# Deformable attention and binary convolution on one core: another order of the first steps, thirteen product buffers, nine DMA sums and another order of projections

## What is computed

```python
# layer 1, deformable attention: 8 heads, 4 points, head size 8
q = x.reshape(B, C, Nq).transpose(0, 2, 1)
v = (q @ W_value + b_value).reshape(B, Nq, HEADS, d)
off = (q @ W_off + b_off).reshape(B, Nq, HEADS, LEVELS, POINTS, 2)
attn = softmax((q @ W_attn + b_attn).reshape(B, Nq, HEADS, POINTS), axis=-1)
loc = ref + off / norm                       # where each point samples v
sampled = bilinear sample of v at loc (0 outside the image)
out = (sampled.reshape(B, HEADS, d, Nq, POINTS) * aw).sum(-1)
x1 = (out @ W_out + b_out + q)               # back to (4, 64, 32, 32)
# layer 2, binary convolution
y = conv3x3(sign(x1 + move0_bias), mean(|w|) * sign(w), padding 1)
y = batchnorm(y) * gamma + beta              # mean and variance over the whole batch
y = prelu(y + x1 + move1_bias) + move2_bias
```

## Time and profile before

| | |
|---|---|
| median of three runs | 86.0 us (85.94 to 86.25) |
| the profiled execution | 85.9 us |
| its span, first to last instruction | 84.1 us |
| PE busy | 66.5 us, 79% |
| DVE busy | 58.7 us, 70% |
| POOL busy | 47.7 us, 57% |
| ACT busy | 46.2 us, 55% |
| mean granted clock of TensorE | 0.951 |

### The profile page before, as it was taken

The page is one execution under the profiler, slowest core; times in us unless marked ns, Lnnn a source line. Parts: engine busy times, 40 slices in busy tenths (PEclk is TensorE's granted clock), DMA queues, the critical chain, the costliest instruction groups (busy, mean ns, idle before and its releaser), DMA issues.

```text
span 84.1 us, 1712 instructions
## 1 busy us (share of the span) xinstructions
PE 66.5 (79%) x642; PEld 25.4 (30%) x642; DVE 58.7 (70%) x85; ACT 46.2 (55%) x92; POOL 47.7 (57%) x47
## 2 busy tenths in 40 slices
PE   5999997999799999999999959999799985200000
PEld 4766275223142322132323314222223542200000
DVE  2307978999989999596997889203970067689920
ACT  2401999995599999997000399900000397059500
POOL 7970000879999999999999999950000000009000
PEclk9999999999999999999999999999999999995555
DMA  0917865920599980091006638390000000000195
GB/s 9 295 42 253 250 232 123 224 74 0 97 207 213 213 146 1 0 216 37 0 8 134 119 53 134 64 189 4 0 0 0 8 0 0 0 4 0 24 281 194
DMA packets 3897, 8.09 MB, mean 96 GB/s; under 512 B 560, under 2 KB 1584, under 8 KB 3888
## 3 DMA queue, kind: packets, MB, share of 16 engines
q1 hardware_dynamic: 2320, 4.40, 19.1%
q0 software_dynamic: 1120, 2.88, 19.0%
q10 hardware_dynamic: 448, 0.69, 2.6%
HBM read 2.27 MB, written 1.05 MB: 39 GB/s over the span
## 4 chain that ended last, share of the span: by engine, by line
PE 50%; DVE 19%; POOL 10%; issue 8%; DMA 5%; ACT 2%; DVEq 1%; ACTq 0%; POOLq 0%
PE banks L530 21%; PE banks L513 12%; POOL ap L864 10%; DVE prod L970 6%; DMA win<-w_in_dram 5%; PE banks L562 4%; PE banks L476 3%; PE banks L508 3%; DVE prod L1104 3%; PE banks L459 2%; DVE prod L1115 2%; DVE bns L1075 2%; ACT sg L783 2%; DVE ays L941 1%; PE banks L466 1%
## 5 line engine op out<-in xcount | busy, mean ns | idle before, releaser
L864 POOL TENSOR_TENSOR ap<-ays,hat 128x512 f32<-128x512 f32 (+2 forms) x30 | 36.1, 1592 | 9.7 <-ACT hat L695 9.2
L970 DVE TENSOR_TENSOR prod<-banks,vpad 128x1024 f32<-128x1024 f32 (+2 forms) x20 | 22.1, 1114 | 8.2 <-PE banks L530 5.1
L530 PE MATMUL banks<-prod,wo 64*64 64x512 f32 (+2 forms) x208 | 23.1, 547 | 0.7 <-PE banks L530 0.5
L513 PE MATMUL banks<-ap,cst 32*64 32x512 f32 (+2 forms) x192 | 16.9, 567 | 1.5 <-POOL ap L864 1.0
L888 POOL TENSOR_SCALAR prod<-prod,prm,st 128x512 f32<-128x512 f32 x3 | 2.3, 763 | 19.8 <-ACT st L831 19.8
L970 DVE TENSOR_TENSOR prod<-banks,vswap 128x1024 f32<-128x1024 f32 (+3 forms) x13 | 12.6, 975 | 0.0
L530 PEld LDWEIGHTS banks<-prod,wo 64*64 64x64 f32 x208 | 6.9, 132 | 15.1 <-issue 11.1
L513 PEld LDWEIGHTS banks<-ap,cst 32*64 32x64 f32 x192 | 4.3, 130 | 13.7 <-POOL ap L864 8.1
L688 ACT ACTIVATE tab<-u,cst 128x512 f32<-128x512 f32 x12 | 8.3, 716 | 0.1
L871 POOL DMA_DIRECT2D prod<-prod x6 | 7.3, 1217 | 0.2 <-ACT hat L695 0.2
L695 ACT ACTIVATE hat<-tab 128x512 f32<-128x512 f32 x12 | 7.2, 621 | 0.0
(11 more groups left out here) (84 smaller groups left out, 79.3 us busy)
## 6 DMA issues: line engine op xcount, KB each, us to landing
prod<-prod POOLq DMA_DIRECT2D x4, 512.0 KB, 5.4
vswap<-vpad SPq DMA_DIRECT2D x4, 432.0 KB, 5.5
xs<-x_dram SPq DMA_DIRECT2D x3, 256.0 KB, 4.2
prod<-prod POOLq DMA_DIRECT2D x2, 384.0 KB, 5.4
out_dram<-prod SPq DMA_DIRECT2D x2, 256.0 KB, 3.2
wcf<-w_conv_dram SPq DMA_DIRECT2D x1, 288.0 KB, 4.2
wab<-w_abs_dram SPq DMA_DIRECT2D x1, 288.0 KB, 4.2
xs<-x_dram ACTq DMA_DIRECT2D x1, 256.0 KB, 2.9
```

Source lines behind the costliest of these rows:

```text
L513: mm = pe.matmul(spread_into(t)[quadrant(i, g, t in SWAPPED)[1], g, 0:size_of(t)], sel_of(g)[rows_in, quadrant(i, g)[1]], weights_at(t)[ro ...
L530: mm = pe.matmul(into, wo[rows_in, rows_in], source, start=False, stop=last, skip_group_check=True)
L864: pool.tensor_tensor(into, factor, near, ALU.mult).then_inc(s_ap, 1)
L970: nc.vector.tensor_tensor(as_window(t, prod[:, t % PR, g, 0:n]), as_window(t, spread_into(t)[:, g, 0:n]), v_window(t, g), ALU.mult).then_i ...
```

## The change

- **First steps.** On PE, `turn(0)` and the bias of logits part 2 come ahead of `values(0)`, and the second half of logits part 2 comes behind `spread(0)`. `values(0)` writes banks 2 and 3 instead of 0 and 1, so `spread(1)` waits until the values are stored. On DVE, `attend(0)` and `weight(0)` come ahead of `store_upper_values`.
- **Who does what.** `DVE_COLUMNS` goes from 2 to 1: weight 1 goes from DVE to POOL. The scaling of softmax part 2 goes from POOL to DVE. `softmax_max(2)` goes behind product 0, the other steps of part 2 behind products 1 and 2. `attend(2)` to `attend(5)` move by one or two products.
- **ACT.** The hat (x, ZERO) comes ahead of the distance (x, MINUS).
- **Buffers and sums.** PR goes from 12 to 13, and the ring of DVE's own weights from 3 to 1. There are nine sums instead of six, over other pairs, and 23 projected units, 11 above and 12 below, in another order. `turn(1)` comes behind spread 4 instead of spread 5.

```diff
-SUM_FROM = {1: 2, 5: 6, 8: 10, 16: 18, 20: 22, 24: 26}
-SUMS_BEHIND = {6: 1, 9: 5, 15: 8, 23: 16, 26: 20, 29: 24}
-DVE_COLUMNS = [2] + [0] * (ROWS - 1)
+SUM_FROM = {0: 1, 8: 2, 12: 10, 5: 4, 13: 9, 18: 16, 26: 24, 25: 17, 20: 22}
+SUMS_BEHIND = {7: 0, 11: 5, 13: 8, 18: 12, 19: 13, 24: 18, 26: 20, 28: 25, 30: 26}
+DVE_COLUMNS = [1] + [0] * (ROWS - 1)
...
-        RA, RAP = 3, 6
+        RA, RAP = 1, 6
...
-        PR = 12
+        PR = 13
...
-        ps_v = [[bank[0], bank[1]], [bank[5], bank[4]]]
+        ps_v = [[bank[2], bank[3]], [bank[5], bank[4]]]
...
-        TAPS_AFTER = {7: [4], 9: [0, 3], 11: [9, 1], 13: [7], 15: [5, 12], 17: [15], 19: [14, 8], 21: [11], 23: [13],
-                      27: [19, 23, 17], 29: [25, 27, 21, 16], 31: [29]}
-        TAPS_AT_END = [24, 28, 30, 20, 31]
+        TAPS_AFTER = {9: [0, 6, 3], 11: [5, 7], 13: [11], 15: [8], 17: [14], 19: [15], 21: [12], 23: [13], 27: [21, 19, 23],
+                      29: [18, 20, 28], 31: [29, 25, 27]}
+        TAPS_AT_END = [30, 26, 31]
...
             offsets(0, 0)
-            values(0)
             pe.wait_ge(s_sub, 2)
             logits_bias(2)
+            pe.wait_ge(s_cst, 16)
+            turn(0)
+            values(0)
             pe.wait_ge(s_x[1], 32)
             logits(2, range(NCH // 2))
-            pe.wait_ge(s_cst, 16)
-            turn(0)
-            logits(2, range(NCH // 2, NCH))
             pe.wait_ge(s_u, 2)
             base_positions(1, 1)
             for taps in SPREADS:
+                if taps[0] == 1:
+                    logits(2, range(NCH // 2, NCH))
+                    pe.wait_ge(s_vp, G)
...
-                if t == 5:
+                if t == 4:
                     turn(1)
...
             hats(0)
+            hats(1)
             distances(2)
-            hats(1)
...
-                pool.wait_ge(s_p, products_done(more, G - 1))
+                pool.wait_ge(s_p, products_done(max(into, more), G - 1))
...
-                if t == 6:
-                    pool.wait_ge(s_rec, 3)
-                    pool.tensor_tensor(grouped(prob[:, 1, :]), grouped(ex[:, 1, :]), spread_points(lrec[:, 1, :]),
-                                       ALU.mult).then_inc(s_prob, 1)
...
             def product(t):
                 yh, ky, kx = tap_of(t)
+                if t == 0:
+                    dve.wait_ge(s_vp, G)
...
-            store_upper_values()
             attend(0)
             weight(0)
-            weight(1)
-            softmax_max(2)
-            ROW_AFTER = [0, 3, 6, 7, 9, 9, 9]
+            store_upper_values()
+            ROW_AFTER = [0, 1, 4, 7, 8, 9, 9]
             for t in range(NT * YH):
                 product(t)
                 if t == 0:
+                    softmax_max(2)
+                if t == 1:
                     softmax_sub(2)
                 if t == 2:
                     softmax_sum(2)
                     softmax_recip(2)
+                    softmax_scale(2)
```

## The result

The changed kernel takes **88.4 us** (median of four runs, 88.04 to 88.99) where the kernel before takes 86.1 beside it (85.94 to 86.89): 1.025 times the time of before, 95% interval 1.017 to 1.034. Forecast were 83.2, with a range of 82.4 to 85.1. The prediction was wrong, in its sign too. The profiled execution of the changed kernel took 88.99, its span is 87.2, and its mean granted clock 0.905, against 0.951. Executions of one and the same kernel fall into faster and slower ones; in what follows a median is over all of them and a ratio over the faster alone, so that kernels with the same median can have different ratios (e1 and e4), and the profiled executions of e5, e7 and e8 were among the slower.

What follows compares the result with a forecast made beforehand. What counts was taken to be when PE reaches the flag, 65.2 us: spread 27 1.0 earlier plus 1.9 in the tail gives 2.9, kept at 2.8, so 86.0 becomes 83.2 us; range 82.4 to 85.1.

Steps and rivals of the forecast that it cites:

- the price of the scaling: On DVE before product 10: the scaling of 512 columns takes 0.6 to 0.7 us, as the reduction.
- signs of being wrong: Spread 27 later than 50.4, PE or DVE waiting over 1 us for a sum's DMA, or clock below 1.00 before the flag.
- The clock: Rival: PE, partly idle between 22 and 27 us, falls to half clock; 87.2 us if 4 us are lost; chance 0.08.
- The start: Up to product 0: it starts at 14.95 instead of 15.45, 0.5 us earlier; weight 1 on POOL costs nothing.
- DVE up to product 10: Maximum and scaling join this stretch: product 10 at 32.4, 16.14 + 1.3 behind product 0, 0.7 to 0.8 us later.
- The loss is gone: At product 12 on DVE: about 34.6 against 34.54 before, since it hardly waits for PE now.
- POOL: Weight 27 waits for the sum of 20 and 22, starts at 47.55, is ready at 49.35; spread 27 is 1.0 us earlier.
- POOL takes over: Rival: dearer, waiting issues make POOL 2 us later, weight 27 ready at 51.3; 85.1 to 86 us; chance 0.12.
- Late sums: Rival: sums land late, delaying products, PE and weight 27 by 0.7 to 1.5 us; 83.9 to 84.7 us; chance 0.20.
- The tail: On PE from spread 27 to the flag: 12.9 us instead of 14.8, 1.9 saved, with spreads 30 and 31 paired.
- Thirteen buffers: Products 28 to 31: product 28 no longer waits for a projection, 5.05 us before, and starts near 53.2.
- products up to 22: PE and DVE hand over, two fewer 512-column units: product 22 at 45.7 against 46.41, 0.7 us earlier.

Runs made afterwards that it cites:

- e1: The changed kernel with the scaling of softmax part 2 back on POOL, behind weight 7 and its sum: 85.7 us, 0.994 of the kernel before.
- e4: The changed kernel with one more wait: POOL does not begin weight 8 before DVE's scaling is done: 85.7 us, 0.988 of the kernel before.
- e5: The changed kernel with ACT writing the exponentials of part 2 into PSUM, so the scaling has one SBUF operand: 84.8 us, 0.979 of the kernel before.
- e7: e5 with the small cast of the positions at the start on ACT instead of DVE: 84.6 us, 0.981 of the kernel before.
- e8: e5 without the sum of 22 onto 20, unit 22 projected among the last: 84.3 us, 0.975 of the kernel before.
- e12: The kernel before with the new sums, thirteen buffers and new order of projections, old first steps, a ring of two weights: 88.8 us, 1.024.
- e10: The changed kernel with DVE's scaling of the lower half cut into four instructions of 128 columns: 88.3 us, 1.020 of the kernel before.

## Why the prediction was wrong, by its own steps

The time-table that it worked out step by step is best held against e5, which is the changed kernel less the stall, and then the changed kernel against e5. Forecast, e5 and after, in us; sections between the same points:

| section | forecast | e5 | after |
|---|---|---|---|
| product 0 | 14.95 | 15.61 | 15.60 |
| product 0 to 10 | 17.45 | 17.55 | 22.07 |
| product 10 to 22 | 13.3 | 13.70 | 13.69 |
| product 22 to weight 27 | 1.85 | 2.04 | 2.04 |
| weight 27 to spread 27 | 1.80 | 2.34 | 1.92 |
| spread 27 to flag | 12.9 | 12.60 | 12.60 |
| flag | 62.25 | 63.84 | 67.92 |

The rows of e5 behind it, DVE (products 10, 12 and 22), POOL (the last sum ahead of weight 27, and that weight) and PE:

```profile
33.16 1.22 DVE L975 TENSOR_TENSOR prod<-banks,vpad 128x1024 f32<-128x1024 f32 x1
...
35.53 1.23 DVE L975 TENSOR_TENSOR prod<-banks,vpad 128x1024 f32<-128x1024 f32 x1 [0.29 <-PE banks L518]
...
46.86 0.96 DVE L975 TENSOR_TENSOR prod<-banks,vpad 128x768 f32<-128x768 f32 x1 [0.39 <-PE banks L518]
```

```profile
48.12 2.03 POOL L878 DMA_DIRECT2D prod<-prod  x1
48.90 2.29 POOL L871 TENSOR_TENSOR ap<-ays,hat 128x384 f32<-128x384 f32 x1
```

```profile
51.24 0.87 PE L518 MATMUL banks<-ap,cst 32*64 32x384 f32 x8 [1.13 <-POOL ap L871]
...
63.84 0.19 PE L526 MATMUL banks<-over,ones 128*1 128x6 f32 x2
```

- **The step that failed is the price of the scaling: "I take 0.6 to 0.7, as the reduction".** It measured 4.07. The reduction reads one operand, from PSUM (`lmax<-banks`), and the scaling two from SBUF, and the prediction compared them by their columns alone. It also gave no upper end: 1.15, POOL's own time, was the largest number in sight. Nor was POOL looked at for what it would be doing in that stretch; before, POOL did this very scaling there, so it could not be in DVE's way. DVE's own weights of before, two operands in SBUF as well, were no warning, for they ran while POOL stood idle until 15.04:

```profile
13.55 1.29 DVE L951 TENSOR_TENSOR a<-ays,hat 128x512 f32<-128x512 f32 x2
```

But the trace of before had a warning, in its last steps, which was overlooked. The elementwise operation L1115 of DVE has two operands in SBUF and takes 0.74; the first of four, which began beside the last of POOL's (L888), took 1.11 and ended at 78.47, 0.54 behind POOL's end:

```profile
77.17 0.76 POOL L888 TENSOR_SCALAR prod<-prod,prm,st 128x512 f32<-128x512 f32 x1
77.36 1.11 DVE L1115 SCALAR_TENSOR_TENSOR prod<-prod,st 128x512 f32<-128x512 f32 x1
78.39 0.74 DVE L1115 SCALAR_TENSOR_TENSOR prod<-prod,st 128x512 f32<-128x512 f32 x1
```

Because of the stall product 3 is 3.38 later than in e5. Two of the prediction's own signs of being wrong showed up with it: spread 27 later than 50.4, and a stretch with a granted clock below 1.00 ahead of the flag.
- **The clock was a rival, at 0.08 and 87.2 us, and half right.** It fell in the predicted stretch. But its cause is the stall, not a DVE fuller by 1.3: in e5, with the same projections and the same order, it stays at 1.00. Its price is 1.1 us instead of 4. The stall itself, 3.4 us, was no part of any rival. The Trainium skill (TensorE: Matmul & The Clock Gate, What's actually happening) says that an idle TensorE falls to half its clock; the trace agrees, with 0.50 from 27 to 33 us behind 3.86 us without work.
- **The start** was right in kind, though not in these two executions (15.60 and 15.61). Over ten executions with the new first steps product 0 starts at 15.2 on average, over six with the old ones at 16.0. The forecast gain of 0.5 held or better. The absolute 14.95 was too early by luck of the draw: 15.45, from which it was counted, was an early one of the old.
- **DVE up to product 10** was right without the stall: 17.55 for 17.45. "The loss is gone" at product 12 was not quite: 35.53 in e5 for 34.6, of which 0.7 is the later product 0.
- **POOL was mis-sized, not misread.** Weight 27 waits for the sum of 20 and 22, as forecast. The issue took 0.78, in the stated bounds of 0.61 to 0.98 (the upper bound was misread: before, the scaling behind that issue also waited for the reciprocal, done at 21.58; an issue without such a wait behind it takes 0.61 or 0.77 to 0.79 in these traces). What is missing is that the weight is ready 2.29 behind its start instead of 1.8; on that growth see the last section. The rival "POOL takes over", at 0.12, has weight 27 ready at 51.3 and 85.1 us. In e5 it was ready at 51.19, and e5 took 84.8. So with the stall out of the way that rival came nearer than the forecast, if partly through the late start of that execution.
- **Late sums** didn't happen in the changed kernel: 4.4 to 6.1 us from issue to landing. They did in e12, for the first sum rather than for those that the prediction watched.
- **The tail** was right, 12.6 for 12.9, with spreads 30 and 31 as a pair (62.26, and 58.17 in e5), product 28 waiting for its spread only, and 184 matmuls in L530. Thirteen buffers do what they were to do.

To add up: e5 misses the forecast flag by 1.6, of which 0.7 is the start of that one execution, 0.5 the longer time of weight 27 on POOL, 0.5 products up to 22, less 0.3 in the tail, and 0.2 the sum's issue. The changed kernel misses e5 by 4.1: 3.4 the stall, 1.1 the clock, less 0.4 that POOL, which had stood still for 3.42 us, gave back at spread 27.

## What to carry to other kernels

Before an operation moves between DVE and POOL, list where each of its operands lies and what the other of the two engines computes at that time; with two operands in SBUF, the price on DVE here was what POOL had left to do without a pause, and one operand in PSUM made it its own length again. Look for such a pair of operations side by side in the whole trace, not only in the stretch that the change touches. Two parts of a change of which one spares the engine that the other loads should be costed together: here each alone was worth nothing or less, and the gain of 2.1% came only with both. A term that is priced from a row of another form needs as its upper end the longest thing that could run beside it.

## What the runs showed of the hardware that was not expected

- **DVE against POOL.** A 512-column multiplication on DVE with both operands in SBUF: 0.69 us with POOL waiting, 1.45 with one weight of POOL under way, 4.07 with three. With POOL under way it ended 0.55 to 0.56 behind it. The 128-column version ended 0.16 behind.
- **For weights it holds for a run of instructions, not for one.** POOL's next weight began before its last one ended, and in e10 DVE wasn't let in between.
- **A cast from SBUF seems to meet it as well**, with one operand only and beside memsets: its ends fall on theirs in 15 traces. That is a coincidence of times: no run moved the memsets to test it, and which property of the cast it would be was not tried. One operand in SBUF alone is not the reason: before, a reduction of 512 columns from SBUF took 0.68 while POOL computed:

```profile
19.75 1.01 POOL L864 TENSOR_TENSOR ap<-ays,hat 128x384 f32<-128x384 f32 x1
19.92 0.68 DVE L909 TENSOR_REDUCE lsum<-ex 128x128 f32<-128x512 f32 x1
```

- **Between the two memsets DVE does get in.** The second begins at 3.80, before the first ends at 3.86. All eleven casts that began by 3.72 ended near 3.9, and all four that began from 3.74 on near 5.86. So the rule of the run, from the weights, does not carry over to every pair of instructions.
- **A weight's time on POOL grows with the sums issued.** The step from the start of one weight of 512 columns to the next stays at 1.22 to 1.27, while the time from a weight's start to its end grows with every sum issued. In e1 (scaling on POOL, no waits after it), weights 25 and 27:

```profile
45.28 2.91 POOL L866 TENSOR_TENSOR ap<-ays,hat 128x512 f32<-128x512 f32 x1
...
48.52 3.12 POOL L866 TENSOR_TENSOR ap<-ays,hat 128x384 f32<-128x384 f32 x1
```

It is 1.28 for a weight of 512 columns ahead of the first sum, and 1.50 behind it (at 22.55 in the changed kernel). PE's waits follow the ends, so the growth is real to others: a sum costs what waits for POOL 0.2 to 0.3 us beyond its visible step, as long as POOL doesn't wait. After a wait it starts afresh: in e8 an issue behind one takes 0.87 and the weight behind it 1.58. It looks like a queue inside POOL that fills up, but no run shows what it is.

```profile
51.11 0.87 POOL L878 DMA_DIRECT2D prod<-prod  x1 [0.40 <-DVE prod L975]
51.72 1.58 POOL L871 TENSOR_TENSOR ap<-ays,hat 128x512 f32<-128x512 f32 x1
```
